# Raw int32 mask tiles loaded by the sync queue into two slots, in place of cast tiles loaded by GpSimd into four

## The reference

```python
# x: (2, 4096, 4096)   weight: (4096, 4096) f32   mask: (4096, 4096) int32, constant in 32x32 blocks
block_mask = mask.reshape(128, 32, 128, 32).astype(f32).sum(axis=(1, 3)) > 0
w_masked = weight * repeat(repeat(block_mask, 32, 0), 32, 1)
x = layernorm(x + einsum('bsk,nk->bsn', x, w_masked))
w = (unpack_int4(weight_packed) - zero_point) * scale
x = layernorm(x + einsum('bsi,oi->bso', x, w) + bias)
```

## Time and profile before

| | us |
|---|---|
| median of 3 runs (1444.88 to 1477.81) | 1448.35 |
| profiled execution, device time | 1450.07 |
| its span, slowest core (core 1) | 1448.5 |
| spans of the 8 cores | 1404.3 to 1448.5 |
| TensorE busy (matmul) | 1026.9, 71% |
| VectorE busy | 750.4, 52% |
| ScalarE busy | 249.6, 17% |
| GpSimd busy | 131.1, 9% |

### The profile page before, as it was taken

The page is one execution under the profiler, slowest core; times in us unless marked ns, Lnnn a source line. Parts: engine busy times, 40 slices in busy tenths (PEclk is TensorE's granted clock), DMA queues, the critical chain, the costliest instruction groups (busy, mean ns, idle before and its releaser), DMA issues.

```text
span 1448.5 us, 11966 instructions; the slowest of 8 cores (1404.3 to 1448.5 us)
## 1 busy us (share of the span) xinstructions
PE 1026.9 (71%) x4468; PEld 424.0 (29%) x4468; DVE 750.4 (52%) x500; ACT 249.6 (17%) x207; POOL 131.1 (9%) x106
## 2 busy tenths in 40 slices
PE   0000859495896898699972569999999999998100
PEld 0000324142342343244420014444444444443000
DVE  4300938574785686586327973333333333332686
ACT  0000000000000000000011014444434344442100
POOL 2000001000000000000008300000000000000453
PEclk9999979798899899799985689999999999998555
DMA  9998458768488489475101002121121212210343
GB/s 144 163 144 132 65 56 126 110 104 131 84 123 140 65 135 130 71 111 67 25 0 59 0 0 85 62 74 71 59 87 59 88 59 74 73 62 27 126 178 160
DMA packets 90232, 127.73 MB, mean 88 GB/s; under 512 B 69664, under 2 KB 69696, under 8 KB 77888
## 3 DMA queue, kind: packets, MB, share of 16 engines
q0 software_dynamic: 13664, 75.52, 32.7%
q10 hardware_dynamic: 9216, 50.34, 9.4%
q1 hardware_dynamic: 67296, 1.11, 2.9%
HBM read 185.16 MB, written 17.30 MB: 140 GB/s over the span
## 4 chain that ended last, share of the span: by engine, by line
PE 47%; DMA 23%; DVE 21%; issue 5%; SPq 1%; ACT 1%; DVEq 0%; POOLq 0%; POOL 0%; ACTq 0%
PE ps L491 30%; PE ps L343 13%; DMA em<-bmx_scr 12%; DMA bmx_scr<-bmtr 8%; DVE crbf L237 7%; DVE scr_bf L290 3%; DVE arena_b L553 3%; DVE em L544 3%; DVE scr_bf L621 2%; DVE em L615 2%; PE ps L313 1%; DMA outT<-scr_bf 1%; PE ps L321 1%; SPq L185 1%; DMA scr_i<-maskn 1%
## 5 line engine op out<-in xcount | busy, mean ns | idle before, releaser
L343 PE MATMUL ps<-arena_a,scr_bf 128*128 128x512 bf16 x2048 | 462.0, 388 | 195.2 <-DVE scr_bf L290 194.9
L491 PE MATMUL ps<-arena_b,scr_bf 128*128 128x512 bf16 x2048 | 461.3, 384 | 53.9 <-DVE arena_b L553 51.2
L343 PEld LDWEIGHTS ps<-arena_a,scr_bf 128*128 128x128 bf16 x2048 | 201.6, 100 | 450.6 <-issue 222.9
L491 PEld LDWEIGHTS ps<-arena_b,scr_bf 128*128 128x128 bf16 x2048 | 196.3, 98 | 318.1 <-issue 92.7
L290 DVE TENSOR_TENSOR scr_bf<-scr_bf,em 128x2048 bf16<-128x2048 bf16 x64 | 143.2, 2276 | 181.2 <-DMA em<-bmx_scr 181.2
L237 DVE TENSOR_REDUCE crbf<-scr_i 128x128 bf16<-128x4096 bf16 x32 | 226.5, 7118 | 13.0 <-DMA scr_i<-maskn 13.0
L365 ACT ACTIVATE mb_b<-arena_b 128x1024 bf16<-128x1024 bf16 x32 | 33.8, 1057 | 542.1 <-DVE arena_b L358 330.2
L468 DVE TENSOR_SCALAR scr_i<-scr_i 128x2048 int32<-128x2048 int32 x32 | 39.3, 1229 | 168.4 <-DMA scr_i<-ptpr 168.4
L516 DVE TENSOR_TENSOR arena_a<-em,arena_b 128x512 bf16<-128x512 f32 x64 | 44.3, 692 | 134.1 <-ACT em L510 134.1
L358 DVE TENSOR_TENSOR arena_b<-ps,arena_a 128x512 bf16<-128x512 f32 x64 | 42.1, 673 | 127.8 <-PE ps L343 127.6
L476 ACT CAST scr_bf<-scr_i 128x2048 bf16<-128x2048 int32 x32 | 60.8, 1899 | 166.4 <-DVE scr_i L468 166.4
(11 more groups left out here) (48 smaller groups left out, 271.5 us busy)
## 6 DMA issues: line engine op xcount, KB each, us to landing
scr_bf<-wtpr POOLq DMA_DIRECT2D x32, 1024.0 KB, 11.1
scr_i<-maskn POOLq DMA_DIRECT2D x32, 1024.0 KB, 20.1
scr_i<-ptpr ACTq DMA_DIRECT2D x32, 1024.0 KB, 4.8
outT<-scr_bf ACTq DMA_DIRECT2D x32, 512.0 KB, 2.7
arena_a<-xT POOLq DMA_DIRECT2D x4, 2048.0 KB, 65.7
bmx_scr<-bmtr SPq DMA_DIRECT2D x64, 8.0 KB, 5.9
em<-bmx_scr SPq DMA_DIRECT2D x16, 32.0 KB, 4.2
sel_s<-sel SPq DMA_DIRECT2D x1, 32.0 KB, 3.4
```

Source lines behind the costliest of these rows:

```text
L343: sp=(ci == C - 1): o.matmul(ps[b_][:, 0:SHW], scr_bf[:, D * (v_ % 4) + 128 * c_: D * (v_ % 4) + 128 * (c_ + 1)], arena_a[:, SC * c_ + SHW ...
L491: lambda o, w_=w, h_=h, c_=c, b_=bk, wo=woff: o.matmul(ps[b_][:, 0:SHW], scr_bf[:, wo: wo + 128], arena_b[:, SC * c_ + SHW * h_: SC * c_ + ...
```

## The change

`mask_stage_a` loads the mask as it is, in int32, by the sync queue: two DMAs for each 128 rows (one for each half of the columns), four for a step. A tile is now 16 KB a partition, so `scr_i32` holds two slots and not four, and the loads of step m wait until the reductions of step m-1 are done. The reduction reads int32 and not bf16. The first steps are put in another order: `xq_load(0)` (a quarter of x) goes ahead of the second weight tile, step 1 of the mask comes after `mask_stage_b(0)` and `wt_mult(0)`, and the other quarters of x come before step 2. The names of the hazards in the second product follow the new slots.

```diff
         def mask_stage_a(m):
             for half in range(2):
                 i = 2 * m + half
-                slot = i % 4
+                slot = i % 2
                 cslot = i % 4
-                msl = mskv[:, D * slot: D * (slot + 1)]
-                dma("gpsimd", "Qm%d" % slot, msl,
-                    t_mask.ap()[128 * i: 128 * (i + 1), :],
-                    writes=[("msl", slot)])
-                def red_fn(o, d=cslot, sl=slot):
-                    mv = bass.AP(mskv, D * sl, [[4 * D, 128], [1, KBN], [KBN, 32]])
+                msl = scr_i32[:, D * slot: D * (slot + 1)]
+                qbase = 2 * slot
+                for hh in range(2):
+                    dma("sync", "Qm%d" % (qbase + hh),
+                        msl[:, (D // 2) * hh: (D // 2) * (hh + 1)],
+                        t_mask.ap()[128 * i: 128 * (i + 1),
+                                    (D // 2) * hh: (D // 2) * (hh + 1)],
+                        writes=[("msl", slot, hh)])
+                def red_fn(o, sl=slot, d=cslot):
+                    mv = bass.AP(scr_i32, D * sl, [[2 * D, 128], [1, KBN], [KBN, 32]])
                         return o.tensor_reduce(crbf[:, KBN * d: KBN * (d + 1)],
                                                mv, AX.X, ALU.add)
-                P("vector", red_fn, reads=[("msl", slot)], writes=[("crb", cslot)])
+                P("vector", red_fn, reads=[("msl", slot, 0), ("msl", slot, 1)],
+                  writes=[("crb", cslot)])
...
         wt_refill(0)
         mask_stage_a(0)
-        if NSL > 1:
-            mask_stage_a(1)
+        xq_load(0)
         if C > 1:
             wt_refill(1)
         mask_stage_b(0)
         wt_mult(0)
-        xq_load(0)
+        if NSL > 1:
+            mask_stage_a(1)
         if C > 2:
             wt_refill(2)
+        for g_ in range(1, NXD):
+            xq_load(g_)
         if NSL > 2:
             mask_stage_a(2)
-        for g_ in range(1, NXD):
-            xq_load(g_)
...
-                writes=[("qsl", slot), ("msl", slot)])
+                writes=[("qsl", slot), ("msl", 0, 0), ("msl", 0, 1)])
...
-              reads=[("qsl", slot)], writes=[("l32",), ("msl", 2)])
+              reads=[("qsl", slot)], writes=[("l32",), ("msl", 1, 0), ("msl", 1, 1)])
...
-              reads=[("qsl", slot)], writes=[("h32",), ("msl", 3)])
+              reads=[("qsl", slot)], writes=[("h32",), ("msl", 1, 0), ("msl", 1, 1)])
```

More of the change, by code:

```diff
@@ L227, in mask_stage_a @@
                 i = 2 * m + half
-                slot = i % 4
+                slot = i % 2
                 cslot = i % 4
-                msl = mskv[:, D * slot: D * (slot + 1)]
-                dma("gpsimd", "Qm%d" % slot, msl,
-                    t_mask.ap()[128 * i: 128 * (i + 1), :],
-                    writes=[("msl", slot)])
-                def red_fn(o, d=cslot, sl=slot):
-                    mv = bass.AP(mskv, D * sl, [[4 * D, 128], [1, KBN], [KBN, 32]])
-                    with nc.allow_low_precision(reason="int 0/1 sums <= 1024 exact in bf16"):
+                msl = scr_i32[:, D * slot: D * (slot + 1)]
[8 more added lines that the diff above has]
+                    mv = bass.AP(scr_i32, D * sl, [[2 * D, 128], [1, KBN], [KBN, 32]])
+                    with nc.allow_low_precision(reason="int 0/1 sums exact"):
                         return o.tensor_reduce(crbf[:, KBN * d: KBN * (d + 1)],
                                                mv, AX.X, ALU.add)
-                P("vector", red_fn, reads=[("msl", slot)], writes=[("crb", cslot)])
+                P("vector", red_fn, reads=[("msl", slot, 0), ("msl", slot, 1)],
+                  writes=[("crb", cslot)])
         def mask_stage_b(m):
```

## The result

Over 12 runs each, the changed kernel takes 1461.26 us in the median and the kernel before 1452.25; the ratio is 1.0081, with a 95% interval of 1.0056 to 1.0107. I had forecast slower, 1500 us. So the sign is right and the size is not: 0.8%, where 3.5% was forecast. A change of 0.8% lies clear of zero here, but it is inside the 2% that the prediction counted as no change; to that outcome it gave 0.24, to slower 0.63. The profiled execution took 1457.88 us, and its slowest core is core 6 with a span of 1456.3. The cores are closer together now, 1435.8 to 1456.3.

The account below looks back on a forecast made before the run. The first product was taken as bound by the block mask's small transfers and reductions; -16.2 us at the start, +76 in the steps, -10 in the tail give +50.2 on 1450.07, forecast 1500, range 1440 to 1555.

Parts of the forecast that it names:

- the ring: First product's steps: transpose, small writes, `em`, masks, reduction and next transpose form a closed chain, nothing prefetched; 41.75 us a step.
- the wait on `em`: VectorE's 18 us wait for the read-back in the steps; claimed to go, with `em` ahead of the masks in one queue.
- Fourteen steps: 584.5 us: First product from step 1's to step 15's transpose: fourteen steps of 41.75 us, ending at 736.2.
- the prediction's one line: Change in the first product's end: -16.2 us at the start, +76 in fourteen steps, -10 in the tail.
- the count of the steps: Step 1 to step 15 of the first product: fourteen intervals, each charged the full 41.75 us.
- The forecast of +50 us: End of the first product: 795.4 us instead of 745.2, +50.2; the second product adds no wait.
- Start: Before the steps: `em` of step 0 at 102.1 us, step 1's transpose at 151.7 instead of 167.86, 16.2 us gained.
- A step: Transpose to transpose in the first product: 6.8 + 3.0 + 19.7 + 0.3 + 7.15 + 4.8 = 41.75 us, against 36.3 before.
- the reduction of int32: VectorE's mask reduction in each step: 7.15 us as in bf16, set by spacing; bounds 4.6 and 14.3 us.
- Rivals A and C: VectorE's mask reduction: A, cheap at 4.6 us, 1456 in all, chance 0.15; C, dear at 14.3 us, 1633, chance 0.06.
- Rival B: Mask loads in the steps do not collide with the weight refill: 34.2 us a step, 1394 in all, chance 0.13.
- The tail: TensorE's last four tiles of the first product after step 15's transpose: 59.2 us, where it was 69.2.

Follow-up runs that it names:

- early_act: Changed kernel with the next step's int32 mask loads issued right behind the reductions, on ScalarE's queue instead of SP's; 1482 us, ratio 1.011.
- early_sp: Changed kernel with the next step's int32 mask loads issued right behind the reductions, still on SP's queue; 1376 us, ratio 0.954.
- early_act_bhalf: Changed kernel with mask loads right behind the reductions on ScalarE's queue, and `mask_stage_b` one tile sooner, behind its tile's matmuls and additions; 1376 us, ratio 0.952.
- before_2slots: Kernel before, cast masks still on GpSimd, with two mask slots instead of four; two runs, 1425 and 1487 us, ratio not measured.

## Why the prediction was right and wrong

The mechanism held: the ring is there, and the wait on `em` is gone. What failed is one term of the sum, "Fourteen steps: 584.5 us". It measured 687.80 - 147.40 = 540.4, so that the +76 us of the prediction's one line were +32.2. Of the 44.1 us too many, 22.4 came from the price of a step and 21.7 from the count of the steps. The forecast of +50 us was the small difference of two large sums (584.5 against 508.2 us for the steps), so these 44 us were most of it; between the two profiled executions the change came out at +7.8. The steps of the working, one by one:

*Start, right.* `em` of step 0 landed just before VectorE began at 105.59 (forecast 102.1), and step 1's transpose came at 147.4 (forecast 151.7). The first wide matmul came at 126.3 and not near 105: the small matmuls of step 1 stand ahead of it on TensorE and wait for the reductions. That was overlooked, and it did no harm, as the reductions were the path.

*A step, right in form, too dear.* Transpose to issue of `em`: 6.1 us (forecast 6.8). From there to the second tile: 21.9 (3.0 + 19.7). Seen by VectorE: 0.1 (0.3). From the start of the reduction to the multiplications: 6.9 (7.15). Multiplications and compare: 4.8 (4.8). Together 39.8, where 41.75 was forecast; over 13 steps 40.0. No single part is far off, but every part that differs was put too high, and 1.72 us thirteen times is 22.4 us, the largest part of the miss. The choice that mattered most, the reduction of int32, was right: 7.05 us, as in bf16. The rule of the Trainium skill's page VectorE: DVE Perf Modes, one element a cycle, from which the prediction estimated 4.3 us, holds for neither type here. The note on cachelines in the Trainium skill's page SBUF — State Buffer fits both, but no run here reduces elements that lie close together, so the cause of the 7 us is not shown. Rivals A and C fall with that row. A's time, 1456, is nearer to the measured 1461 than mine, but by luck: its reduction of 4.6 us took 7.05. Rival B falls with the step of 40.0: the refill did collide, at 6.5 us.

*The count of the steps, wrong.* Between the transposes of steps 14 and 15 there is no reduction, since `mask_stage_a(15)`, the last, is reduced at v = 24, ahead of the transpose of step 14 at v = 25. So 13 intervals go round the ring, and the fourteenth runs at TensorE's pace: 20.0 us, not 41.75. The row for it was at hand in the kernel before, whose last interval is 18 us (to 676.03) and whose steps from 1 to 14 are therefore 37.7 us on its slowest core and not the 36.3 I took over all:

```profile
657.96 0.30 DVE L257 STREAM_TRANSPOSE bmtr<-bmb 32x128 bf16<-32x128 bf16 x1
```

The prediction asked what a step costs with care and how many there are without any.

*The tail*, 59.2 us by forecast, took 70.2 (69.2 in the kernel before), as TensorE is still behind with the tiles of the last interval. That gives back 11.0 of the 21.7 us that the count was off: with the interval it is 90.2 for 101.0. So with the right count alone the forecast would still have been some 1490.

The sum: -4.3 (start) - 22.4 (13 steps of 1.72) - 10.8 (last interval and tail) = -37.5 us, which brings the forecast end of the product from 795.4 to 757.9; it is at 757.96. A further 4.9 us were gained behind it, from there to the end of the span: 698.3 us, 703.3 before. Of these, 3.9 lie in the last stage, from the end of the second product's matmuls to the end of the span, 115.6 us for 119.5. The runs tell two things of this stage. It takes 118.1 to 119.5 us on each of the 40 cores of the five kernels that cast their masks, and 114.3 to 117.0 on each of the 72 cores of the nine kernels with int32 masks; and it does so wherever the first product ends, from 650 to 860 us. So this gain goes with the changed code and not with the moment at which a core arrives. The code of that stage is the same in both and the names of the hazards differ before it; what in the code does it stays open. The -37.5 us above and these -4.9 are the 42.4 us between 1500.3 and the profiled 1457.88.

*What the slowest core hides.* In the kernel before the waits on `em` hit the cores unequally: step 14 comes at 615 us on core 7 and at 658 on core 1. In the changed kernel all cores go round the same ring, 648 to 668. The median of the cores' spans went from 1423 to 1447, some 24 us, the slowest only from 1448.5 to 1456.3, so a typical core lost three times as much as the metric shows. I worked from the slowest core alone, which is right for the metric, and said nothing of the others.

*Where the gain went.* The change does remove the waits on `em`, for which TensorE idled 15 to 19 us in five of its steps before, by putting it ahead of the masks in one queue. It gives them back: TensorE now idles 25 us in the first of the 13 steps and 6.3 to 9.6 in each of the others (8.8 and 8.3 us ahead of the tiles at 272.1 and 312.3 in its timeline). The order in a queue is what the Trainium skill's page DMA: Bandwidth & Descriptors, section on queues, rings and completion order, describes: on an engine of the DMA system a ring's descriptors are taken in their order, and the engine goes round between rings. The traces agree: behind no mask in its own queue `em` lands in 3.9 us (median, changed kernel); with masks in another queue and a weight refill beside it in up to some 30 (`early_act`, and before).

## What to carry to other kernels

Before you price a ring, write down for every index which instruction stands between which two, to the last one: the ring ends when its last load does. A queue of their own does not protect small transfers from large ones in another queue. Either put both in one queue and the small one that is waited for ahead of the next large ones (`em` in `early_sp`), or start the small ones so early that their slow landing is waited for by nobody (`early_act_bhalf`); both were worth nearly 5%. And when a load is moved to a queue that waits in its midst, look at what it stands behind: issuing the same loads on the same queue right after the reductions that free their slots took the changed kernel from a ratio of 1.008 to 0.954. On ScalarE's queue the same move won nothing by itself (1.011).

## What the runs showed of the hardware that I had not expected

Sixteen-byte runs in one queue crawl beside full-size transfers in another, with GpSimd as with ScalarE as the issuer of those: the read-back of 32 KB takes 3.9 us ahead of the masks in its own queue, and up to 30.6 beside int32 masks from ScalarE's queue and a weight refill from GpSimd's. A reduction over elements 128 apart costs 1.74 ns an element in bf16 and 1.72 (7049 / 4096) in int32, so at these spacings (256 and 512 bytes) the width of the element does not enter. Halving the slots of a prefetch (`before_2slots`) made the profiled execution faster than any of the seven runs of the kernel before in its batch (1425 against 1439 at least), and less was loaded ahead of what was wanted first; its second run took 1487, so this is an indication only.
